# Grouped whitening of 32 images on one core: a new step order with the weights folded in, 128-partition stores from SyncE, and transposes of 768 columns

## The reference, cut to what matters

```python
x1 = x.reshape(N, C // G, G, H, W).transpose(0, 2, 1, 3, 4).reshape(N, G, -1)
mean = x1.mean(-1, keepdims=True)
xc = x1 - mean
cov = xc @ xc.transpose(0, 2, 1) / M + EPS * jnp.eye(G, dtype=x.dtype)
Y = cov / norm(cov); Z = eye(G)
for _ in range(10):
    T = 0.5 * (3.0 * I - Z @ Y)
    Y = Y @ T
    Z = T @ Z
decorr = Z / jnp.sqrt(norm(cov))
y = weight1 @ decorr @ xc + bias1
```

## Time and profile before

| what | us |
| --- | --- |
| runs | 467.77, 476.04, 463.84 |
| median | 467.77 |
| the profiled execution | 462.93 |
| its span, first to last instruction | 461.0 |
| around the span | 1.93 |

### The profile page before, as it was taken

The page is one execution under the profiler, slowest core; times in us unless marked ns, Lnnn a source line. Parts: engine busy times, 40 slices in busy tenths (PEclk is TensorE's granted clock), DMA queues, the critical chain, the costliest instruction groups (busy, mean ns, idle before and its releaser), DMA issues.

```text
span 461.0 us, 17013 instructions
## 1 busy us (share of the span) xinstructions
PE 379.3 (82%) x7392; PEld 271.3 (59%) x7392; DVE 329.4 (71%) x1033; ACT 332.9 (72%) x450; POOL 56.8 (12%) x108
## 2 busy tenths in 40 slices
PE   0868899898989899898989897989999897977700
PEld 0856766666657667675756665666767575633100
DVE  5767887797869777988868787779888786643000
ACT  5772478797969868787878787787878796455800
POOL 0000001111111111020111111111102011112500
PEclk9976999999999989999989999899999999999965
DMA  7999939999999999999999999999999666677990
GB/s 271 416 409 410 412 141 284 338 346 351 381 358 404 357 394 344 398 390 390 385 383 362 381 394 382 367 327 388 384 391 388 218 208 208 200 213 225 312 268 18
DMA packets 28747, 152.11 MB, mean 330 GB/s; under 512 B 3968, under 2 KB 3968, under 8 KB 20736
## 3 DMA queue, kind: packets, MB, share of 16 engines
q0 software_dynamic: 9952, 75.50, 46.6%
q1 hardware_dynamic: 18432, 75.51, 43.2%
q10 hardware_dynamic: 288, 0.01, 0.0%
HBM read 75.51 MB, written 75.50 MB: 328 GB/s over the span
## 4 chain that ended last, share of the span: by engine, by line
PE 67%; DVE 11%; ACT 8%; issue 5%; DMA 2%; POOL 1%; SPq 0%; DVEq 0%; POOLq 0%; ACTq 0%
PE cov_ps L432 29%; PE y_ps L493 25%; PE chain_ps L464 6%; ACT image L220 6%; DVE transposed L315 5%; PE chain_ps L462 2%; DMA image<-x 2%; PE cov_ps L444 1%; PE chain_ps L474 1%; POOL y L188 1%; DVE yz L353 1%; DVE t_mat L354 1%; DVE col L350 1%; ACT image L230 1%; PE chain_ps L466 1%
## 5 line engine op out<-in xcount | busy, mean ns | idle before, releaser
L315 DVE STREAM_TRANSPOSE transposed<-image 128x384 f32<-128x384 f32 x384 | 215.7, 572 | 13.5 <-ACT image L220 2.8
L230 ACT ACTIVATE image<-y_ps,y_bias 128x768 f32<-128x768 f32 x192 | 164.8, 894 | 68.4 <-PE y_ps L493 67.7
L432 PE MATMUL cov_ps<-transposed 128*64 128x65 f32 x4608 | 178.7, 231 | 5.4 <-issue 5.4
L493 PE MATMUL y_ps<-image,apply_w 64*64 64x384 f32 x1536 | 171.8, 513 | 4.4 <-issue 2.3
L432 PEld LDWEIGHTS cov_ps<-transposed 128*64 128x64 f32 x4608 | 160.9, 142 | 14.5 <-issue 6.3
L220 ACT ACTIVATE image<-image,shift 128x1152 f32<-128x1152 f32 x128 | 156.1, 1248 | 1.8 <-DMA image<-x 0.8
L493 PEld LDWEIGHTS y_ps<-image,apply_w 64*64 64x64 f32 x1536 | 58.9, 135 | 15.1 <-ACT image L230 7.6
L186 POOL DMA_DIRECT2D y<-image x34 | 19.4, 572 | 381.1 <-ACT image L230 381.1
L462 PEld LDWEIGHTS chain_ps<-yz 128*64 128x64 f32 (+1 forms) x288 | 32.8, 138 | 35.4 <-DVE yz L367 27.3
L367 DVE SCALAR_TENSOR_TENSOR yz<-yz,chain_ps 64x96 f32<-64x96 f32 x144 | 33.8, 234 | 22.9 <-PE chain_ps L464 16.9
L464 PE MATMUL chain_ps<-yz,t_mat 64*64 64x96 f32 x256 | 47.0, 265 | 3.4 <-DVE t_mat L362 3.4
(11 more groups left out here) (59 smaller groups left out, 167.1 us busy)
## 6 DMA issues: line engine op xcount, KB each, us to landing
image<-x SPq DMA_DIRECT2D x128, 576.0 KB, 11.2
y<-image POOLq DMA_DIRECT2D x31, 1152.0 KB, 8.6
y<-image POOLq DMA_DIRECT2D x62, 576.0 KB, 11.0
y<-image POOLq DMA_DIRECT2D x3, 384.0 KB, 12.2
y<-image POOLq DMA_DIRECT2D x6, 192.0 KB, 11.6
b_col<-bias ACTq DMA_DIRECT2D x4, 0.1 KB, 6.3
w_nat<-weight ACTq DMA_DIRECT2D x2, 4.0 KB, 4.3
```

What stands on the lines that cost most here:

```text
L230: nc.scalar.activation(xs[n % SLOTS][:, :, STRIP * q:STRIP * (q + 1)], y_ps[:, f % 2, :, 0:STRIP], ACT.Identity, bias=y_bias[:, c % 2, i:i ...
L315: nc.vector.transpose(xt[q][:, TILES // 2 * part:TILES // 2 * (part + 1), 0:CH], xs[n % SLOTS][:, h, at:at + TWELFTH]).then_inc(transposed, 1)
L432: ins = nc.tensor.matmul(cov_ps[rows, n % 2, 0:GRAM], xt[q][:, t, 0:CH], xt[q][:, t, 0:GRAM], start=q == 0 and t < 2, stop=q == IMAGE_PIEC ...
L493: ins = nc.tensor.matmul(y_ps[out_rows, f % 2, h, 0:STRIP], apply_w[rows, c % 2, i].rearrange("p k g -> p (k g)"), xs[n % SLOTS][rows, h, ...
```

## The change

- Steps: the last Newton step, the folding in of the weights and the spread are merged. The weights' transpose `w_t` lies beside y and z in one tile `wyz`; step LAST multiplies z with w_t and y at once, and the matmul of SPREAD applies the last factor. The chain goes from 23 steps (0 to 22) to 21 (0 to 20).
- Order: NORM goes to slot 2 on PE and slot 4 on DVE, NEXT_0 to slot 5, each later step one slot after the other, SPREAD again to slot 23. ACT's root goes behind the pass's first output piece, its second root into round 2. The bias product (`offset`) leaves SPREAD and goes to slot 0 of the next pass, with semaphores of its own; ACT's first output waits for it. GATHER gets one more matmul and one more copy (`means`).
- Output: the matmuls put rows 0 to 63 of both halves into one PSUM bank and rows 64 to 127 into the other, so that nothing is swapped: `xs[:, r]` holds, in partition 64 o + p, channel 128 o + 64 r + p.
- Stores: two transfers an image, of all 128 partitions by 9216 bytes, into channels o = 0, 1 by p = 0 to 63. SP issues them, on the queue of the loads; load n + 9 is issued behind store n and waits for store n - 1.
- Transposes: two of 768 columns in a round (slots 0 and 2) in place of four of 384.

The diff, cut to its core:

```diff
-FOLD = NEXT_0 + 1 + 2 * (NEWTON - 1)
-SPREAD = FOLD + 1
-STEP_AT = {1: NORM, 3: NEXT_0} | {t + 1: t for t in range(NEXT_0 + 1, SPREAD + 1)}
+LAST = NEXT_0 + 1 + 2 * (NEWTON - 2)
+SPREAD = LAST + 1
+OFFSET_AT, NORM_AT, NORM_OUT_AT, NEXT_0_AT = 0, 2, 4, 5
+PE_AT = {NORM_AT: NORM} | {NEXT_0_AT + t - NEXT_0: t for t in range(NEXT_0, SPREAD + 1)}
+DVE_AT = {NORM_OUT_AT: NORM} | {NEXT_0_AT + t - NEXT_0: t for t in range(NEXT_0, SPREAD + 1)}
...
-    out_v = out.rearrange("n (h p) a b -> n p h (a b)", h=HALVES)
+    out_v = out.rearrange("n (o r p) a b -> n r o p (a b)", o=HALVES, r=2)
...
         def _(sp):
-            for n in range(IMAGES):
+            def load(n):
                 for p in range(QUARTERS):
                     h, o = p // ROW_PARTS, p % ROW_PARTS
                     if n >= SLOTS and o == 0:
-                        sp.wait_ge(stored[n % SLOTS][h], 16 * (1 + h) * (n // SLOTS))
+                        sp.wait_ge(stored[n % SLOTS][h], 16 * (n // SLOTS))
                     sp.dma_start(quarter_of(n, p), x_v[n, :, h, QUARTER * o:QUARTER * (o + 1)]).then_inc(
                         loaded[n % SLOTS][p], 16)
+            def store(n, pieces):
+                sp.wait_ge(y_read, IMAGE_PIECES * n + pieces.stop)
+                cols = slice(STRIP * pieces.start, STRIP * pieces.stop)
+                for r in range(2):
+                    sp.dma_start(out_v[n, r, :, :, cols], xs[n % SLOTS][:, r, cols]).then_inc(stored[n % SLOTS][r], 16)
+            for n in range(SLOTS):
+                load(n)
+            for n in range(IMAGES):
+                if n == IMAGES - 1:
+                    for q in range(0, IMAGE_PIECES, 2):
+                        store(n, slice(q, q + 2))
+                else:
+                    store(n, slice(0, IMAGE_PIECES))
+                if 0 < n and n - 1 + SLOTS < IMAGES:
+                    load(n - 1 + SLOTS)
...
-            def store(n, pieces):
-                pool.wait_ge(y_read, IMAGE_PIECES * n + pieces.stop)
-                cols = slice(STRIP * pieces.start, STRIP * pieces.stop)
-                slot = xs[n % SLOTS]
-                pool.dma_start(out_v[n, :, 0, cols], slot[:, 0, cols]).then_inc(stored[n % SLOTS][0], 16)
-                for rows, channels in ((slice(0, HALF), slice(HALF, P)), (slice(HALF, P), slice(0, HALF))):
-                    pool.dma_start(out_v[n, channels, 1, cols], slot[rows, 1, cols]).then_inc(stored[n % SLOTS][1], 16)
...
-                nc.vector.transpose(xt[q][:, TILES // 2 * part:TILES // 2 * (part + 1), 0:CH],
-                                    xs[n % SLOTS][:, h, at:at + TWELFTH]).then_inc(transposed, 1)
+                nc.vector.transpose(xt[q][:, :, 0:CH], xs[n % SLOTS][:, h, at:at + PIECE]).then_inc(transposed, 1)
...
+                elif t == LAST:
+                    weighted, product = product, chain_ps[0:Q, C_PRODUCT + G:C_PRODUCT + 2 * G]
+                    link(nc.vector.scalar_tensor_tensor(
+                        out=t_wide[:], in0=product.unsqueeze(1).to_broadcast([Q, 2, G]), scalar=-0.5, in1=eye15_wide[:],
+                        op0=ALU.mult, op1=ALU.add))
+                    link(nc.vector.scalar_tensor_tensor(
+                        out=folded[:], in0=weighted.unsqueeze(1).to_broadcast([Q, PAIR, G]), scalar=RSQ, in1=own,
+                        op0=ALU.mult, op1=ALU.mult))
...
                 for row in range(2):
                     for half in range(2):
                         rows, out_rows = slice(HALF * row, HALF * (row + 1)), slice(HALF * half, HALF * (half + 1))
-                        h = row ^ half
-                        ins = nc.tensor.matmul(y_ps[out_rows, f % 2, h, 0:STRIP], apply_w[rows, c % 2, i].rearrange("p k g -> p (k g)"),
-                                               xs[n % SLOTS][rows, h, STRIP * q:STRIP * (q + 1)], start=True, stop=True)
+                        ins = nc.tensor.matmul(y_ps[out_rows, f % 2, row, 0:STRIP],
+                                               apply_w[rows, c % 2, i].rearrange("p k g -> p (k g)"),
+                                               xs[n % SLOTS][rows, half, STRIP * q:STRIP * (q + 1)],
+                                               start=True, stop=True)
```

More of the change, by code:

```diff
@@ L168, in _ @@
                     if n >= SLOTS and o == 0:
-                        sp.wait_ge(stored[n % SLOTS][h], 16 * (1 + h) * (n // SLOTS))
+                        sp.wait_ge(stored[n % SLOTS][h], 16 * (n // SLOTS))
                     sp.dma_start(quarter_of(n, p), x_v[n, :, h, QUARTER * o:QUARTER * (o + 1)]).then_inc(
                         loaded[n % SLOTS][p], 16)
+            def store(n, pieces):
[13 more added lines that the diff above has]
+                    load(n - 1 + SLOTS)
+            for n in range(SLOTS):
+                for r in range(2):
+                    stores = (IMAGES - n + SLOTS - 1) // SLOTS + (IMAGE_PIECES // 2 - 1 if n == (IMAGES - 1) % SLOTS else 0)
+                    sp.wait_ge(stored[n][r], 16 * stores)
         @block.gpsimd
@@ L258, in _ @@
                         output(before, f)
[L259 removed]
+                    if j == 2 and exists(c - 1):
                         half_root(c - 1)
@@ L291, in _ @@
             dve.wait_ge(shift_mat_ready, 1)
-            for zeros in (yz, t_mat, parity):
+            for zeros in (wyz, t_mat, parity, means):
                 then(nc.vector.memset(zeros[:], 0.0))
@@ L302, in _, with transpose @@
             then(nc.vector.tensor_scalar(eye15[:], eye[0:Q, 0:Q], 1.5, None, ALU.mult))
[L303 to L311, removed]
+            then(nc.vector.tensor_scalar(eye15_wide[:], eye_col[0:Q, :].unsqueeze(1).to_broadcast([Q, 2, G]), 1.5, None,
+                                         ALU.mult))
+            then(nc.vector.tensor_scalar(mean_mat[:], eye_col[:].unsqueeze(1).to_broadcast([P, 2, G]), 1.0 / SAMPLES,
+                                         None, ALU.mult))
+            def transpose(n, q):
+                h, at = q // PIECES, PIECE * (q % PIECES)
+                dve.wait_ge(centred, QUARTERS * n + (PIECE * (q + 1) - 1) // QUARTER + 1)
+                if n > 0:
                     dve.wait_ge(cov_done, IMAGE_PIECES * (n - 1) + q + 1)
-                h, at = k * TWELFTH // PIXELS, k * TWELFTH % PIXELS
-                nc.vector.transpose(xt[q][:, TILES // 2 * part:TILES // 2 * (part + 1), 0:CH],
-                                    xs[n % SLOTS][:, h, at:at + TWELFTH]).then_inc(transposed, 1)
+                nc.vector.transpose(xt[q][:, :, 0:CH], xs[n % SLOTS][:, h, at:at + PIECE]).then_inc(transposed, 1)
             def covariance_out(n):
@@ L398, in _ @@
                     j = s // SLOTS_A_ROUND
-                    if s in STEP_AT and exists(c - 1):
-                        chain(c - 1, STEP_AT[s])
+                    if s == OFFSET_AT and exists(c - 2):
+                        offset(c - 2)
+                    if s in DVE_AT and exists(c - 1):
+                        chain(c - 1, DVE_AT[s])
                     if s == 9 and exists(c):
@@ L408, in _ @@
                     n = PAIR * c + (j + 2) // 3
-                    if n < IMAGES:
-                        transpose(n, (4 * j + 8) % TWELFTHS + s % SLOTS_A_ROUND)
+                    if n < IMAGES and s % 2 == 0:
+                        transpose(n, (2 * j + 4) % IMAGE_PIECES + s % SLOTS_A_ROUND // 2)
         @block.tensor
@@ L506, in _ @@
                         covariance(PAIR * c + 2 * j // IMAGE_PIECES, 2 * j % IMAGE_PIECES)
-                    if s in STEP_AT and exists(c - 1):
-                        chain(c - 1, STEP_AT[s], slice(0, P) if exists(c) else slice(0, Q))
+                    if s == OFFSET_AT and exists(c - 2):
+                        offset(c - 2)
+                    if s in PE_AT and exists(c - 1):
+                        chain(c - 1, PE_AT[s], slice(0, P) if exists(c) else slice(0, Q))
                     ahead = PAIR * c + 1 + j // 3
@@ L514, in _ @@
                     for m in range(1, SLOTS_A_ROUND):
-                        if s + m in STEP_AT and exists(c - 1):
-                            chain(c - 1, STEP_AT[s + m], slice(0, Q))
+                        if s + m in PE_AT and exists(c - 1):
+                            chain(c - 1, PE_AT[s + m], slice(0, Q))
                         if m < 3 and exists(c - 2):
```

113 lines of the change are left out of this document (54 added, 59 removed).

## The result

The changed kernel takes 1605.47 us (median of 4 runs, 1604.08 to 1605.77), the kernel before 467.82 (4 runs, 463.84 to 476.04). The ratio is 3.441, with a 95% interval from 3.420 to 3.462. The profiled execution took 1604.08 us, its span 1602.3.

A forecast was written before the change was run, and what follows sets the result against it. Compute order was taken as the bound before, with DMA close behind. With stores on two engines: 69 to the first store + 1430 stores + 123 loads + 4 = 1626, plus 1.93 around the span, say 1630 us; range 1575 to 1760.

The forecast's parts named there:

- The number of engines: New stores: an outermost count of 2 on one side lets only two engines carry all 75.5 MB; chance 0.83.
- The packets of before: POOL's queue before: 9952 packets, of which 7936 rows, 1632 completions and 384 for the last image's nine transfers.
- The rate of one engine: Stores: each of two engines moves 26.4 GB/s, so 37.75 MB each takes 1430 us.
- The loads: Loads sharing the stores' queue: 22 images after the first store put 3.25 MB on each engine, 123 us.
- The start: Before the first store: issued at 68.9 us, with this part of the kernel changing by 1 or 2 us at most.
- When compute starts to wait: Passes: the two engines never dry up, and compute waits for them from the fourth or fifth image on.
- The view of after: Profile after: DMA share near 0.22, some 93 GB/s, stores landing after 45 us, two completions a transfer, PE under 40%.
- the other parts: Order, transposes, fewer chain steps, clock and stores' end: count only if stores run on 16 engines, otherwise hidden behind DMA.
- the 16-engine rival: Stores: all 16 engines carry them, since dealing goes by row; 426 us, from 410 to 448; faster, chance 0.12.
- The order and transposes: Compute passes: a gain of 1.5 us in each of 14 full passes, 21 us; at the low end 0.
- The idle in front of NEXT_0: First round of a pass: PE's 1.66 us wait shrinks to 0.6 to 0.9 us, gaining 0.8 to 1.1.
- The end of the run: After ACT's last piece: 128-row stores cut 15 us to some 7, and 8 of 9 idle us go; 16 together.

The follow-up runs named there:

- the version with four transfers of 64 rows: The changed kernel with each 128-partition store cut into two transfers of 64 rows, all on SP's queue: 440.53 us, ratio 0.945.
- the version by SP: The kernel before with only the issuer of its three store transfers an image changed, from POOL to SP: 455.62 us, ratio 0.978.

## Why the prediction was right, point by point

- **The number of engines.** The step that decided: both sides of a transfer need an outer count that 16 engines can share, and the new destination has 2. Two completions a transfer, a share of 0.126, and then four engines for a count of 4 show it. The paragraph "How many engines (k)" in the Trainium skill's "DMA: Bandwidth & Descriptors" was what made me trust the step over "all transfers here use 16"; the runs on SP's queue agree with it for 2, 4, 64 and 128.
- **The packets of before.** The prediction took the 384 packets that were left for the rows of the last image's nine transfers. These have 3 x 128 + 6 x 64 = 768 rows, so on POOL's queue two of its rows of 3072 bytes must go in one packet; on SP's queue each row is a packet. The 16 completions a transfer stand, and nothing else hung on the 384.
- **The rate of one engine.** I took 26.4 GB/s; stores alone ran at 26.8. So 37750/26.8 = 1409 us for the stores where I had 1430. This term is the main part of the 25 us by which I was over.
- **The loads.** A cycle of 49.6 us less 1180/26.8 = 44.0 for the store leaves 5.6 us for a load, as forecast: 22 of them are 123 us.
- **The start.** I kept 68.9 us to the first store and allowed 1 or 2 us; in the changed kernel it is issued at 65.78. With 65.8 + 1409 + 123 + 4 and 1.8 around the span the sum is 1604, and the profiled execution took 1604.08. The 4 us at start and end are still an estimate.
- **When compute starts to wait.** "From the fourth or fifth image on" holds only if images stored are counted: ACT's first long wait begins at 112.6 us, for the load of the eleventh image, when about five have been put out. Ten images are loaded before the stores begin. It changed nothing, since only the DMA engines set the end.
- **The view of after.** Forecast: DMA share 0.22 and 93 GB/s; measured 0.252 and 94. The bytes were right, so the engines other than the two were busy for longer with the loads than the 5.7 us an image that I gave them: by an estimate (two engines full over the whole span, the rest of 0.252 shared by 14) some 7 us. Packets, ACT's wait for loads and PE under 40% (26%) came as said, and so did the low clock: the mean granted clock was 0.63. That a store lands after 45 us can't be read on this page, which gives no landing time for these stores; the cycle of 49.6 us stands for it.
- **Not decided by this change: the other parts.** They stood under the 16-engine rival, and hidden behind the stores they had no part in the result. Two of their terms were mis-sized. The order and transposes were put at 1.5 us a pass, 21 us; measured, about 10 in all (467 x 0.021), and in the profiled execution only 2 of its 5.5 us came in twelve of the passes. An undisturbed pass went from 24.29 us to 24.0, and to 23.2 with narrow transposes: the order alone is worth 1.1 us in it, and the wide transposes, put at a gain of 0 to 0.14 us each for DVE, cost 0.8 of that. The timeline of the version with four transfers of 64 rows, one pass of PE and ACT:

```profile
227.13 0.24 PE L485 MATMUL chain_ps<-wyz,t_mat 64*64 64x32 f32 x1 [0.88 <-DVE t_mat L366]
228.46 0.24 PE L487 MATMUL chain_ps<-wyz 64*64 64x32 f32 x1 [0.36 <-DVE wyz L371]
...
222.63 2.40 ACT L231 ACTIVATE image<-image,shift 128x1152 f32<-128x1152 f32 x2
...
246.64 1.25 ACT L231 ACTIVATE image<-image,shift 128x1152 f32<-128x1152 f32 x1
```

The idle in front of NEXT_0 shrank from 1.66 to 0.88 us, as forecast (0.6 to 0.9), but the step behind it now waits 0.36. The end of the run was put at 16 us and gave 10: the 9 us without work behind the last packet went, with POOL no longer storing, but of the 7 us that stores of 128 rows should save there nothing is seen, as the version by SP still has two transfers of 64 rows in three.

## What to carry to other kernels

Before a transfer's shape is changed, write down the outermost count of both sides: on SP's queue a count of 2 gave 2 DMA engines, 4 gave 4, and 64 and 128 gave 16. "128 partitions" on one side says nothing if the other side starts with 2. The completions on the page check it in one line: packets less rows, divided by transfers. Where the two sides can't be given one stride, cut the transfer into several that have it; it costs some instructions on SP, and here it was the difference between 1605 and 440 us.

A second habit: look at the length of an undisturbed pass beside the run's time. The transposes' two widths give the same time within the spread, but not the same pass.

## What the runs showed that was not expected

- The number of engines sets the price while the stores are the bound: alone, they ran at 53.7 GB/s on two engines and 107 on four, 26.8 an engine both times, and the kernel took 1605 and 911 us. On 16 engines it took 440, and there the stores are no longer the bound by themselves.
- The same shape on POOL's queue is 591 us, not 1605: a store lands after 42.3 us, yet several engines beyond two share the work. The queue shows 59328 packets without rows.
- Stores of 64 rows, of both halves of the partitions and with no load beside them, moved 367 GB/s, where the trace before had a stretch at 221.
- An output piece's four matmuls on four quarters of the array against two quarters: 0.90 us and 1.44 us of PE (172.3 and 276.9 us over 192).
- 9 us at the end belonged to POOL having issued stores: the kernel before and the changed one with its stores end with 9.0 and 9.5 us without work, the one with the same transfers by SP with less than 1.
